# Full attention on one Trainium2 core: maxima come out negated, ScalarE empties the banks of turned maxima and outputs, GpSimd multiplies by the reciprocals

## The reference

```python
q = (x @ Wq.T + bq).reshape(b, s, NHEADS, DK)
k = (x @ Wk.T + bk).reshape(b, s, NHEADS, DK)
v = (x @ Wv.T + bv).reshape(b, s, NHEADS, DV)
w = jnp.einsum('bshd,bzhd->bhsz', q, k)
w = w / jnp.sqrt(jnp.float32(DV))
w = jax.nn.softmax(w, axis=-1)
vw = jnp.einsum('bhsz,bzhd->bshd', w, v)
```

## Time and profile before

| | us |
|---|---|
| three runs: lowest, median, highest | 2055.79, 2058.5, 2059.46 |
| profiled execution: span from first to last instruction | 2056.4 |
| full attention, first reduction to last division | 958.2 to 1637.7 |

### The profile page before, as it was taken

How to read it: one execution, slowest core, us unless ns; L and a number is a source line. 1 busy time by engine, 2 the same in 40 slices (tenths; PEclk the granted TensorE clock), 3 DMA queues, 4 the chain that set the end, 5 groups by cost and what they waited for, 6 DMA issues and landing times. The chain is left out here.

```text
span 2056.4 us, 34421 instructions
## 1 busy us (share of the span) xinstructions
PE 1579.5 (77%) x11512; PEld 917.7 (45%) x11512; DVE 1339.0 (65%) x3318; ACT 1135.7 (55%) x2965; POOL 550.2 (27%) x615
## 2 busy tenths in 40 slices
PE   6799999999991699245999999999999735424910
PEld 3478777777771699221222222222222234323910
DVE  5655656656564322267999999999999287842523
ACT  3366766666651344142688888888888733111300
POOL 2133323524526400571001001001000020372056
PEclk9799999999995799666899999999999967556965
DMA  5144311211101676142000000000000000013832
GB/s 191 39 156 156 107 30 36 54 28 43 42 21 37 203 234 205 52 122 83 23 21 26 18 26 18 27 18 26 19 25 2 1 0 6 21 45 124 253 91 72
DMA packets 86203, 138.99 MB, mean 68 GB/s; under 512 B 18084, under 2 KB 57252, under 8 KB 85900
## 3 DMA queue, kind: packets, MB, share of 16 engines
q1 hardware_dynamic: 62860, 92.08, 15.2%
q0 software_dynamic: 11936, 34.49, 5.1%
q10 hardware_dynamic: 11232, 10.23, 1.4%
HBM read 75.51 MB, written 45.11 MB: 59 GB/s over the span
## 5 line engine op out<-in xcount | busy, mean ns | idle before, releaser
L2062 DVE TENSOR_REDUCE q_max<-s_ps 128x1 f32<-128x1024 f32 x512 | 598.2, 1219 | 14.0 <-PE s_ps L1953 6.8
L2043 ACT ACTIVATE probs<-s_ps 128x512 f32<-128x512 f32 x1024 | 535.5, 603 | 124.5 <-PE s_ps L1974 124.3
L1953 PE MATMUL s_ps<-k_stack,q_stack 64*128 64x512 bf16 x1024 | 351.2, 397 | 16.9 <-PEq L96 8.5
L1974 PE MATMUL s_ps<-q_stack,k_stack 64*128 64x512 bf16 x1024 | 319.5, 384 | 20.2 <-ACT probs L2043 15.8
L1988 PE MATMUL o_ps<-probs,v_aug 128*32 128x512 f32 x2048 | 273.6, 606 | 0.7 <-ACT probs L2043 0.7
L1974 PEld LDWEIGHTS s_ps<-q_stack,k_stack 64*128 64x128 bf16 x1024 | 78.6, 94 | 333.9 <-ACT probs L2043 281.9
L989 POOL TENSOR_TENSOR probs<-probs,p_rsum 128x512 f32<-128x512 f32 x128 | 132.9, 1038 | 325.8 <-DVE p_rsum L966 325.1
L869 ACT ACTIVATE probs<-s_biased,s_min 128x128 f32<-128x128 f32 (+1 forms) x512 | 197.7, 391 | 37.0 <-DVE s_min L960 35.6
L734 PE MATMUL score_ps<-k_pad,q_bd 128*128 128x128 f32 x1024 | 146.7, 287 | 0.0
L960 DVE CUSTOM_DVE_ANT_0 s_biased<-score_ps,nbias 128x128 f32<-128x128 f32 (+1 forms) x512 | 115.8, 282 | 41.8 <-PE score_ps L734 40.6
L1580 POOL CAST neg_max_parts<-neg_max 16x128 bf16<-16x128 f32 x32 | 9.0, 281 | 474.7 <-DVE neg_max L2070 474.7
(11 more groups left out here) (315 smaller groups left out, 2824.5 us busy)
## 6 DMA issues: line engine op xcount, KB each, us to landing
moe0b_wblock<-in_L_ffn_blocks SPq DMA_DIRECT2D x39, 578.0 KB, 3.9
moe_rows<-zero_rows POOLq DMA_DIRECT2D x18, 960.0 KB, 4.4
moe1b_wblock<-in_L_ffn_blocks SPq DMA_DIRECT2D x39, 256.0 KB, 3.5
v_shift<-v_tiles SPq DMA_DIRECT2D x32, 256.0 KB, 3.1
v_shift<-v_tiles SPq DMA_DIRECT2D x32, 224.0 KB, 3.6
qk_parts_dram<-qk_parts SPq DMA_DIRECT2D x16, 384.0 KB, 2.7
q_stack<-qk_parts_dram SPq DMA_DIRECT2D x192, 32.0 KB
k_stack<-qk_parts_dram SPq DMA_DIRECT2D x192, 32.0 KB
```

Of the source, the lines that this page charges most:

```text
L1953: mm = nc.tensor.matmul(s1[u % 2][:, c * CH:(c + 1) * CH], qs[head_rows(m), quad % 4, j, qt * P:(qt + 1) * P], ks[head_rows(m), quad % 4, ...
L1974: nc.tensor.matmul(bank_of("exp", 4 * k + pos)[:], ks[head_rows(m), quad % 4, j, kt * P:(kt + 1) * P], qs[head_rows(m), quad % 4, j, half ...
L2043: nc.scalar.activation(pr[:, k % 2, HEADS[pos], :], bank_of("exp", n)[:], ACT.Exp).then_inc(sm["exp"], 1)
L2062: v.tensor_reduce(mx[:, h % 4, col:col + 1], s1[u % 2][:], AX.X, ALU.max).then_inc(sm["maxed"], 1)
```

## The change

DVE's reduction gets `negate=True`, so `q_max` holds negated maxima. The turned maxima are copied out of their bank by ACT (`copy_max`), after the first exponential of the step that follows the turning. The turned output is copied out of its bank by ACT into a new buffer `o_rows` of two halves (`output_rows`), after the second exponential of the step that follows the turning. DVE takes the reciprocals from that buffer one step later than that (`invert_sums`), and GpSimd multiplies (`scale_output`), in an order with `split_max` written out by hand. The order of the ring and PE's stream are as before; `m_neg` and `o_done`, which free the banks, are now given by ACT.

```diff
 # GpSimd
+                def scale_output(m):
+                    pool.wait_ge(sm["o_rsum"], m + 1)
+                    nc.gpsimd.tensor_tensor(
+                        K.nat[:, t:t + CPT, s * 32:(s + 1) * 32].rearrange("p t (h d) -> p t h d", d=HD1),
+                        on[:, m % 2, :, :, 0:HD1], bc(ro[:, m % 2], 3, HD1), ALU.mult).then_inc(sm["o_scaled"], 1)
...
+                    if quad >= 2:
+                        scale_output(2 * quad - 3)
                     if quad >= 1:
                         split_max(2 * quad - 1)
+                        scale_output(2 * quad - 2)
                     split_max(2 * quad)
+                scale_output(2 * NQ - 3)
                 split_max(2 * NQ - 1)
+                scale_output(2 * NQ - 2)
+                scale_output(2 * NQ - 1)
 # ScalarE
+                def copy_max(h):
+                    act.wait_ge(sm["m_turned"], h + 1)
+                    if h >= 1:
+                        act.wait_ge(sm["m_split"], 4 * h)
+                    nc.scalar.copy(nm[:], turned_view(bank_of("m_neg", h))[0:HU, 0, :]).then_inc(sm["m_neg"], 1)
+
+                def output_rows(m):
+                    act.wait_ge(sm["o_turned"], m + 1)
+                    if m >= 2:
+                        act.wait_ge(sm["o_scaled"], m - 1)
+                    nc.scalar.copy(on[:, m % 2].rearrange("p t h c -> p (t h c)"), bank_of("o_done", m)[:]
+                                   ).then_inc(sm["o_done"], 1)
+
+                copy_max(0)
                 for k in range(NK):
                     for pos in range(4):
...
+                        if pos == 0 and k >= 1 and max_done_at(k - 1) is not None:
+                            copy_max(max_done_at(k - 1))
+                        if pos == 1 and k >= 1 and output_due_at(k - 1) is not None:
+                            output_rows(output_due_at(k - 1))
...
                 output(2 * NQ - 1)
+                output_rows(2 * NQ - 1)
 # VectorE
-                    v.tensor_reduce(mx[:, h % 4, col:col + 1], s1[u % 2][:], AX.X, ALU.max
+                    v.tensor_reduce(mx[:, h % 4, col:col + 1], s1[u % 2][:], AX.X, ALU.max, negate=True
                                     ).then_inc(sm["maxed"], 1)
-                def negate_max(h):
...
-                def divide(m):
...
+                def invert_sums(m):
+                    dve.wait_ge(sm["o_done"], m + 1)
+                    v.reciprocal(ro[:, m % 2], on[:, m % 2, :, :, HD1]).then_inc(sm["o_rsum"], 1)
...
-                    if max_done_at(k) is not None:
-                        negate_max(max_done_at(k))
-                    if output_due_at(k) is not None:
-                        divide(output_due_at(k))
-                divide(2 * NQ - 1)
+                    if k >= 2 and output_due_at(k - 2) is not None:
+                        invert_sums(output_due_at(k - 2))
+                invert_sums(2 * NQ - 1)
```

More of the change, by code:

```diff
@@ L1765 @@
             "m_stored", "m_loaded",
-            "s2_mm", "exp", "v_aug", "pv_mm", "o_out", "o_turned", "o_done", "o_rsum")
+            "s2_mm", "exp", "v_aug", "pv_mm", "o_out", "o_turned", "o_done", "o_rsum", "o_scaled")
 def full_attention_stage(nc, K, A, wo, M):
@@ L1823, in full_attention_stage @@
         osb = K.sb("o_sb", [P, 2, CH], ctx=st)
+        on = K.sb("o_rows", [P, 2, CPT, 4, 32], ctx=st)
         mx = K.sb("q_max", [P, 4, 2 * TPB], ctx=st)
@@ L1925, in split_max @@
                            nr[:])
+                def scale_output(m):
+                    quad, half = divmod(m, 2)
+                    b, s = divmod(quad, QUADS)
+                    pool.wait_ge(sm["o_rsum"], m + 1)
+                    t = b * TPB + half * CPT
+                    nc.gpsimd.tensor_tensor(
+                        K.nat[:, t:t + CPT, s * 32:(s + 1) * 32].rearrange("p t (h d) -> p t h d", d=HD1),
+                        on[:, m % 2, :, :, 0:HD1], bc(ro[:, m % 2], 3, HD1), ALU.mult).then_inc(sm["o_scaled"], 1)
                 wo.gate(pool)
@@ L2046, in _ @@
                             output(k // TPB - 1)
+                        if pos == 0 and k >= 1 and max_done_at(k - 1) is not None:
+                            copy_max(max_done_at(k - 1))
+                        if pos == 1 and k >= 1 and output_due_at(k - 1) is not None:
+                            output_rows(output_due_at(k - 1))
+                if max_done_at(NK - 1) is not None:
+                    copy_max(max_done_at(NK - 1))
                 output(2 * NQ - 1)
+                output_rows(2 * NQ - 1)
             @block.vector
@@ L2061, in reduce_max @@
                     dve.wait_ge(sm["m1_mm"], u + 1)
-                    v.tensor_reduce(mx[:, h % 4, col:col + 1], s1[u % 2][:], AX.X, ALU.max
+                    v.tensor_reduce(mx[:, h % 4, col:col + 1], s1[u % 2][:], AX.X, ALU.max, negate=True
                                     ).then_inc(sm["maxed"], 1)
-                def negate_max(h):
[L2067 to L2071, removed]
-                def divide(m):
[L2075 to L2084, removed]
+                def invert_sums(m):
+                    dve.wait_ge(sm["o_done"], m + 1)
+                    v.reciprocal(ro[:, m % 2], on[:, m % 2, :, :, HD1]).then_inc(sm["o_rsum"], 1)
                 for u in range(AHEAD):
                     reduce_max(u)
-                    if u == HU:
-                        negate_max(0)
                 for k in range(NK):
```

## The result

The changed kernel takes 2116.5 us (median of 4 runs, 2110.8 to 2120.6) against 2058.4 us before: ratio 1.0281, 95% interval 1.0267 to 1.0296. It is slower by 58 us; 52 us were forecast, in a range that holds the result. The profiled execution's span is 2113.4 us, 57.0 more than before.

What follows compares the result with a forecast made beforehand. It took a 2.39 us ACT-PE chain, not DVE, as the bound. 39.7 + 14.0 - 2.7 + 0.7 = 51.7 us on a 2056.4 us span gives 2108.1, with 2.1 for the median 2110 us; range 2095 to 2126.

Steps and rivals of the forecast that it cites:

- the 2.39 us chain: Plain step: closed chain through ACT and PE, exponential 3 to score 2, product, score 3, next exponential 3; DVE has no part.
- The copy of the outputs: Step 2: copy behind exponentials 0 and 1 frees score 2's bank 1.28 us later; 31 times, 39.7 us; bounds 1.18 and 1.40.
- the 50 us that the prediction named as a sign: PE's wait for ACT should grow by about 50 us, with the copy of `o_rows` as its releaser.
- The copy of the maxima: Step 5: copy behind exponential 0 makes score 2 start 0.45 us later; 31 times, 14.0 us; bounds 0.41 and 0.54.
- Division off DVE: DVE between reductions around the division: loses 1.07 us now, little saved as the first-pass matmul stands behind; no direct gain counted.
- reciprocals: On DVE after step 3's reductions: cost zero, at most 0.09 us; step 3's present 0.09 us excess should go, -2.7 us.
- negation: In DVE's reduction: taken as zero, at most 0.278 us; rival of a slower negated reduction, 2119 us, chance 0.03.
- GpSimd: Multiplication of about 0.45 us once a half, covered by some 40 us before its buffer is needed: zero.
- After the last step nothing hides anything: End of the kernel: copy 0.58, reciprocal 0.26, multiplication 0.45 in place of reciprocal 0.26, multiplication 0.29: +0.7 us.
- The late maxima: Rival: loads of the maxima reach the loaded half's first score too late, up to 0.5 us more a half, 2125; chance 0.08.
- The ring did bite: Denies the rival that the next score finds another bank free, so copies fit ACT's idle time: 2055 to 2060, chance 0.04.
- DVE's pace: Rival: DVE's occupied time holds the loop, so a half loses 1.10 us: 34 us faster, 2024 us; chance 0.06.

Runs made afterwards that it cites:

- The dose between: Changed kernel with ACT's copy of the turned output after exponential 0 of step 2 instead of exponential 1: 2094.0 us against 2058.0 for the kernel before, ratio 1.0174.
- spare first passes: Changed kernel with first-pass matmuls that nobody reads going on in the last 9 steps: 2112.4 us, ratio 1.0263 to the kernel before.
- the outputs only: Changed kernel with the maxima negated on DVE as before, keeping only the outputs' part: 2100.1 us against 2057.1 for the kernel before, ratio 1.0215.

## Why the prediction was right

*What bounds the kernel.* Right. That DVE does not is shown by the plain step of 2.39 us with its reductions halved; the last half, which the prediction calls the proof, only suggested it, as PE has no first passes there either. That the place of a reader decides, and not its work, is shown by the changed kernel's time coming back without any work coming off an engine. The links of the 2.39 us chain were read from rows; none of them was shortened in a run of its own.

*The copy of the outputs.* Forecast 1.28 us a half, measured 4.27 - 2.97 = 1.30. The dose between, one exponential less, was expected at 3.77 us and measured 3.77. PE's wait for ACT in the stretch grew by more than the 50 us that the prediction named as a sign: by 72.0 us, the waits for the two copies included, 14.0 of which stood before as its wait for the division.

*The copy of the maxima.* Forecast 0.45, measured 3.06 - 2.61 = 0.45; the copy takes 0.24 us where 0.26 was taken between two rows.

*Division off DVE, reciprocals, negation, GpSimd.* All costed at nothing, apart from the 0.09 us of step 3; measured 0.08, the negation 1 ns, and no effect of GpSimd that shows (2115.4 us with the multiplication back on DVE, 2116.5 in the changed kernel). DVE's time around the division became a wait of 0.93 us for the first pass, as the step on the division said.

*The sum.* Forecast 51.7 us, measured 57.0 in the spans and 58 in the medians. The loop's terms came to 52.1. The end behind the last exponential, forecast at 0.7, cost 0.8. What the sum lacked is a term for the granted clock: that the wait of 1.8 us, put into the last half, is followed by 13 us at a granted clock of 0.50. The 31 x 1.28 us counted the last half like every other, and "After the last step nothing hides anything" only the serial work behind it, so the last half's steps were taken as plain, as they are in the earlier trace rows. That left out 4.9 us in the profiled execution. No bound was made for it: the range holds the result because its upper end leaves 9 us for a longer copy and a later DVE, neither of which came, and that part is luck.

*The rivals.* The late maxima did not come: the view of waits from 1000 to 1600 us has no wait of PE for that load. The ring did bite, the negation is free (1220 ns against 1219), and DVE's pace was refuted by the halved reduction (a plain step of 2.39 us still).

## What to carry to other kernels

Where engines hand banks round in a fixed ring, ask which write the emptied bank releases, and what stands ahead of its reader. Here the reader's place in its own stream was the price, more than its duration: a copy of 0.59 us made step 2 last 4.27 us behind two exponentials and 2.97 us behind none. DVE was 96% busy in the kernel before and still followed a loop of latencies that passes by it; look for a stretch where an engine's work is missing and see whether the step is shorter there. Put work that moves between engines first where the receiving engine already waits: the copy of the output put before exponential 0 of step 2, where ACT had waited 0.31 us, cost nothing that the median shows (2056.6 us against 2057.1).

## What the runs showed of the hardware that was not expected

In the loop PE waits 1.8 us in every half for the copied bank and the granted clock is 1.00 over the stretch from 1000 to 1600 us. In the last half, where the first passes are gone, the same wait is followed by a clock of 0.50 from 1671 to about 1684 us, 4.9 us lost; with spare first passes the clock stays 1.00 behind that wait of 1.8 us; and behind a wait of 1.3 us, with the copy one exponential earlier, it stays 1.00 too and all steps are plain ones of 2.39 us. Between the profiled executions of these kernels, then, the same wait of 1.8 us cost the last half 4.9 us in the changed kernel, without first passes on PE, and nothing with spare ones. How long the fall lasts is not settled by the wait alone: behind the same wait it was 13 us in the changed kernel, about 7 us with the multiplication back on DVE and about 3 us with the outputs only (4.9, 2.5 and 1.3 us lost). What sets its length stays open.
